# First layer's attention: max with zero on GpSimd, one more unit of lag, square split 320 to 1728 columns

## The reference, cut to what matters

```python
sq = q2 + swapaxes(k2) - 2.0 * einsum('bhqd,bhkd->bhqk', Q, K)
dist = sqrt(maximum(sq, 0.0))
W = (1e-4 + dist) ** (-2)
W = W / (1e-4 + sum(W, axis=-1, keepdims=True))
A = einsum('bhqk,bhkd->bhqd', W, V)
```

## Time and profile before

| | us |
|---|---|
| median of 3 runs | 7800.41 (7792.85 to 7807.29) |
| span of the profiled execution | 7789.6 |
| VectorE busy | 7317.2 (94%) |
| ScalarE busy | 7213.7 (93%) |
| TensorE busy | 4179.2 (54%) |
| GpSimd busy | 66.0 (1%) |
| stretch of the first layer's attention | 240 to 2720 |

### The profile page before, as it was taken

The page is one execution under the profiler, slowest core; times in us unless marked ns, Lnnn a source line. Parts: engine busy times, 40 slices in busy tenths (PEclk is TensorE's granted clock), DMA queues, the critical chain, the costliest instruction groups (busy, mean ns, idle before and its releaser), DMA issues. The chain is left out here.

```text
span 7789.6 us, 58667 instructions
## 1 busy us (share of the span) xinstructions
PE 4179.2 (54%) x17232; PEld 1286.2 (17%) x17232; DVE 7317.2 (94%) x6415; ACT 7213.7 (93%) x4385; POOL 66.0 (1%) x68
## 2 busy tenths in 40 slices
PE   6666666666766675444444444444444444444445
PEld 3221222222222141111111111111111111111112
DVE  7899999999999858999999999999999999999996
ACT  3799999999999836999999999999999999999996
POOL 0000000000000000000000000000000000000000
PEclk8888888888787886655656656655665655655667
DMA  3100000000000031000000000000000000000002
GB/s 127 39 17 12 16 16 12 16 12 16 12 17 11 28 129 49 10 6 6 10 6 6 10 6 6 10 6 6 10 6 6 10 6 6 10 6 6 10 2 67
DMA packets 113664, 148.32 MB, mean 19 GB/s; under 512 B 17038, under 2 KB 98857, under 8 KB 112634
## 3 DMA queue, kind: packets, MB, share of 16 engines
q1 hardware_dynamic: 104314, 138.54, 5.8%
q10 hardware_dynamic: 9216, 8.39, 0.3%
HBM read 91.55 MB, written 55.31 MB: 19 GB/s over the span
## 5 line engine op out<-in xcount | busy, mean ns | idle before, releaser
L716 PE MATMUL psS<-q_stack,k_stack 102*128 102x512 bf16 (+1 forms) x4096 | 1743.2, 521 | 1979.7 <-DVE work L1023 1128.6
L738 PE MATMUL psO<-work,v_tile 128*32 128x512 f32 x8192 | 1432.7, 822 | 1467.9 <-DVE work L1045 1451.8
L1023 DVE TENSOR_SCALAR work<-psS 128x1024 f32<-128x1024 f32 x1024 | 1203.6, 1219 | 104.7 <-PE psS L716 49.7
L907 DVE SCALAR_TENSOR_TENSOR work<-work,psS 128x1024 f32<-128x1024 f32 x1024 | 1244.5, 1216 | 41.9 <-ACT work L865 41.3
L1066 DVE TENSOR_TENSOR work<-work 128x2048 f32<-128x2048 f32 x512 | 1143.6, 2296 | 77.1 <-ACT work L985 76.8
L865 ACT ACTIVATE work<-psS 128x1024 f32<-128x1024 f32 x1024 | 1100.6, 1075 | 71.2 <-PE psS L716 46.1
L1030 DVE TENSOR_TENSOR work<-work 128x2048 f32<-128x2048 f32 x512 | 1147.7, 2283 | 0.0
L880 ACT ACTIVATE work<-work 128x2048 f32<-128x2048 f32 x512 | 1005.8, 1964 | 0.4 <-ACT ffn_out L797 0.4
L990 ACT ACTIVATE work<-work 128x4096 f32<-128x4096 f32 x256 | 923.9, 3609 | 27.4 <-DVE work L1066 23.6
L980 ACT ACTIVATE work<-work 128x4096 f32<-128x4096 f32 x256 | 910.8, 3606 | 31.2 <-DVE work L1030 21.7
L985 ACT ACTIVATE work<-work 128x2048 f32<-128x2048 f32 x512 | 935.9, 1898 | 1.4
(11 more groups left out here) (124 smaller groups left out, 2478.3 us busy)
## 6 DMA issues: line engine op xcount, KB each, us to landing
qk_parts<-work SPq DMA_DIRECT2D x64, 384.0 KB, 3.2
q_stack<-qk_parts SPq DMA_DIRECT2D x384, 64.0 KB, 2.2
k_stack<-qk_parts SPq DMA_DIRECT2D x384, 64.0 KB, 2.2
ffn_in<-xT_store SPq DMA_DIRECT2D x64, 128.0 KB, 2.5
y_store<-ffn_out ACTq DMA_DIRECT2D x64, 128.0 KB, 1.7
work<-y_store SPq DMA_DIRECT2D x8, 1024.0 KB, 12.2
work<-in_x SPq DMA_DIRECT2D x1, 4096.0 KB, 14.3
xn_store<-work SPq DMA_DIRECT2D x1, 4096.0 KB, 13.0
```

Of the source, the lines that this page charges most:

```text
L716: last = nc.tensor.matmul(m.psS[half][:, q * 512:(q + 1) * 512], m.k_stack[b][0:rows, kt * P:(kt + 1) * P], m.q_stack[b][0:rows, c:c + 512 ...
L738: last = nc.tensor.matmul(m.psO[b][VW * q:VW * (q + 1), :], m.v_tile[b][:, kt, :], ring[:, u % RING, q * 512:(q + 1) * 512], start=kt == 0 ...
L907: nc.vector.scalar_tensor_tensor(part, part, 0.5 / SHEP_EPS, m.psS[half][:, :], ALU.add, ALU.mult).then_inc(s_y, 1)
L1023: nc.vector.tensor_scalar(ring[:, u % RING, half * 1024:(half + 1) * 1024], m.psS[half][:, :], COS_MAX, -COS_MAX, ALU.min, ALU.max)\
```

## The change

In the first layer's attention the max with zero leaves VectorE's loop. GpSimd's queue gets it: for each unit it waits until both quotients of the unit are done and then applies min with the largest fp32 number and max with zero to the whole slot, in place. The two value copies of a head now stand in GpSimd's queue ahead of units 2 and 12. `LAG_INV`, `LAG_SQ` and `LAG_PV` each grow by one. `ACT_SQ` falls from 992 to 320, so that VectorE squares 1728 columns and ScalarE 320. GpSimd's loop over heads is written out for both layers, where a hardware loop ran over the inner heads.

```diff
-    LAG_PV = 5
-    LAG_INV, LAG_SQ = 2, 3
+    LAG_PV = 6
+    LAG_INV, LAG_SQ = 3, 4
-    ACT_SQ = 992
+    ACT_SQ = 320
...
+            def value_tile(h, b, first):
+                if not first:
+                    pool.wait_ge(s_pv, UNITS * h + KT * b + KT - UNITS)
+                nc.gpsimd.tensor_copy(m.v_tile[b][:, :, 0:DH], values[:, b, :, h, :]).then_inc(s_vt, 1)
+
             def head(h, first, last):
...
+                if L == 1:
+                    for b in range(B):
+                        value_tile(h, b, first)
+                else:
+                    for u in range(UNITS):
+                        if u == 2:
+                            value_tile(h, 0, first)
+                        if u == 12:
+                            value_tile(h, 1, first)
+                        c = UNITS * h + u
+                        pool.wait_ge(s_y, 2 * c + 2)
+                        slot = ring[:, u % RING, :]
+                        nc.gpsimd.tensor_scalar(slot, slot, F32_MAX, 0.0, ALU.min, ALU.max).then_inc(s_m, 1)
+            for h in range(HEADS):
+                head(h, h == 0, h == HEADS - 1)
...
                         if u < UNITS:
                             quotient(u, 0)
-                        if u <= UNITS and not (first and u < 1):
-                            dve.wait_ge(s_y, 2 * c)
-                            slot = ring[:, (u - 1) % RING, :]
-
-                            nc.vector.tensor_scalar(slot, slot, 0.0, None, ALU.max).then_inc(s_m, 1)
                         if u < UNITS:
                             quotient(u, 1)
```

More of the change, by code:

```diff
@@ L41 @@
 COS_MAX = 0.999
+F32_MAX = 3.4028234663852886e38
 PI = 3.141592653589793
```

## The result

The change makes the kernel slower: 7854.64 us, median of 4 runs (7847.75 to 7862.06), against 7799.3 for the kernel before (median of 4, 7792.85 to 7807.29). The ratio is 1.0074 with a 95% interval of 1.0059 to 1.0088, so +55 us where -84 was forecast. The predicted 7716 is off by 139 us and the sign is wrong.

The account below looks back on a forecast made before the run. VectorE, full at 4.57 us a unit, was taken to set the pace. The block was to fall from 76.81 to 74.1 us, -87 over 32 blocks, +3 for the end of the stage, from 7800.4: 7716 us, range 7630 to 8020.

Parts of the forecast that it names:

- the extras: VectorE's work between units: 0.39 us per hidden square and 1.21 for `dve_out`, 2.0 together where they were 2.6.
- a max of up to 2.4 us costs nothing: GpSimd's max lies beside the next two quotients, with 2.47 us until the next square; 2.0 us was assumed.
- 4.13 + e: Unit time with an extra e on VectorE, used when it exceeds 4.34 + e/2; 4.13 us is VectorE's own unit.
- the slow rival: GpSimd's max at 3.2 us and VectorE's square alternate and bound the unit at 5.1 us: 8003 us, chance 0.31.
- the forecast's own case: Likeliest case, chance 0.51: max of 2.0 us hidden beside quotients, block 74.1 us, total 7716 us.
- The wait between the quotients: VectorE idles before the second quotient because ScalarE's half isn't there: 0.21 us a unit, around 100 us in all.
- The plain unit: Attention unit without extras: 4.34 us at the fast clock (0.66), 4.62 at the lower (0.34), mixed to 4.44.
- the loop: From first quotient to next unit's second: T + g at least 5.68 us; T is the unit, g its quotients' distance.
- The lag: One unit more of lag costs 0; if its cover failed, 1 to 1.9 us a block, at most 60 us.
- The clock: TensorE's granted clock, 0.83 of full, keeps its share; leaving 0.8 to 0.9 would show the prediction wrong.
- went ahead of the slot's square: Rival: the max gets in before VectorE's square, which stands still; unit about 6.1 us, total 8590, chance 0.03.
- The drain: At the stage's end the last unit passes GpSimd and the longer square, and one more unit stands behind: +3 us.

Follow-up runs that it names:

- experiment 4: Changed kernel with GpSimd's max cut to 32 of the 2048 columns, waits and order kept: 7711.92 us, ratio 0.9893 to the kernel before.
- Experiments 1: Changed kernel with a block's two hidden squares moved from VectorE to ScalarE (kt 3 and 6): 7708.84 us, ratio 0.9892 to the kernel before.
- experiment 5: Kernel before with the three lags one larger and nothing else: 7794.03 us, ratio 0.9998 to the kernel before.
- experiment 3: Changed kernel with the hidden square ahead of the slot's square, behind the second quotient: 7860.87 us, ratio 1.0087 to the kernel before.
- experiment 7: Changed kernel with the hidden square replaced by a one-operand multiplication by 1.0 in place: 7830.15 us, ratio 1.0050 to the kernel before.
- experiment 8: Changed kernel with the hidden square written as relu(x) times x, second operand read from PSUM: 7743.09 us, ratio 0.9935 to the kernel before.

## Why the prediction was wrong, step by step

**The step that failed** is in the paragraph on the extras: "0.39 for each `hidden` square". I took it as 0.6 us of VectorE's time of which part falls into idle time. It was 2.3 us from start to start (1524.86 to 1527.16), because it stands directly behind the slot's square, with no quotient between them, and there GpSimd's max takes its turn. That a max of up to 2.4 us costs nothing, as the prediction has it, holds only where two quotients follow the square; at kt 4, 6 and 8 something else follows it. The prediction's own formula for an extra e too large for the idle time, 4.13 + e, gives 6.43 with e = 2.3, and units 4 and 6 took 6.43 and 6.42. Against the kernel with the short GpSimd operation (experiment 4) units 4 to 7 are 3.77 us longer, 120 us in 32 blocks, and unit 8, where the last product of `dve_out` waits in the same way, 0.59, which is 19: 139 us, the size of the miss. Experiments 1 and 4 remove the squares' wait in two different ways and land at 7709 and 7712. The rows for it were there: in the earlier trace rows a copy gets in between two products that stand back to back and the second pays. I priced that for the slow rival only, as a matter of GpSimd's speed, and I never asked which VectorE instruction stands behind the square in the forecast's own case.

**The rival that it resembles**, a bound on GpSimd, didn't happen. The max wasn't slow: 1.89 us alone (the first one of the stage), 1.76 behind a square, in the forecast's 1.6 to 2.1. It didn't bound the plain unit, and no slot's square waited in the steady state. What the list of rivals lacks is a fast operation in a place with no room. The last product of `dve_out` is the smaller case of it: 0.6 us a block, which the prediction also priced for the slow rival only.

**What held.** VectorE's square cost 1.87 from start to start (1522.99 to 1524.86), as worked out. The wait between the quotients appeared: 175.7 us idle, 174.7 of it released by ScalarE, where 100 was expected; with the short GpSimd operation 157 remain. The plain unit was forecast at 4.44 as a mean over the clock and measured at 4.41 in units 10 to 14. The granted clock there is 0.88 and not 0.83, and the prediction's mix of 4.34 and 4.62 gives 4.41 for it; in experiment 4 the clock there is 0.93, the mix 4.38 and the measured unit 4.38. What was wrong in it is that the low clock was spread evenly: the granted clock is 0.72 in units 4 to 9. The plain unit isn't even, though: the loop says g of the next unit is at least 2.68 less g of this one, and with VectorE never under 1.13 the units alternate, 4.13 and 4.56, whose mean is the 4.34 of the fast clock. The block without the missed term is 74.01 (experiment 4) for 74.1. The lag was free (experiment 5). The clock stayed within 0.8 to 0.9. GpSimd never went ahead of the slot's square: its record starts some 0.17 us after the square's. Where it came up before that square, in experiment 3, it did go ahead.

**Who waits for whom.** A VectorE product with two SBUF operands waited for the max (experiment 3, 3.64 us), a one-operand multiplication in the fast form did too (experiment 7, 2.11), and a product with one operand in PSUM did not (experiment 8, 0.68). SBUF — State Buffer of the Trainium skill (Who interferes with whom) says the same: VectorE instructions with two SBUF inputs contend with GpSimd instructions that read SBUF, `tensor_scalar` can run in a 2-port mode and then contends too, and an instruction with one SBUF input outside these modes does not. The max took 1.76 us behind a square and 1.89 alone; the estimate in the prediction from GPSIMD Engine Reference of the Trainium skill (Elementwise — side-by-side cycle accounting) was 1.76.

**The drain** was forecast at +3 and is 4.7 us longer. In it five slot squares follow one another, and the last max, recorded from 2756.07 for 3.54 us, gets in between two of them, as this row of the changed kernel shows: 11.12 us, where 5 x 1.87 + 0.08 would be 9.4.

```profile
2755.90 11.12 DVE L936 TENSOR_TENSOR work<-work 128x1728 f32<-128x1728 f32 x5
```

**What stays open.** In the changed kernel GpSimd got in between two neighbouring products 64 times of 64; in the earlier trace rows a copy that came up in the middle of a product was passed over by the next one. That row is the exception: of the 28 copies of the kernel before's second layer that came up during one product with another right behind it, 25 got in between and the second product took 2.48 us, and three were passed over. What decides it was not tried.

## What to carry to other kernels

When work moves to GpSimd, list every VectorE instruction that needs both operands from SBUF or runs in the fast form, and look at what stands directly behind each: here a short one behind a long one cost the whole of GpSimd's operation, fast as that was. Reading one operand from PSUM, or moving the short one to ScalarE, removed it. And when a step is taken out from between two others, compare the new distance of the consumers with that of their producers on the other engine; here the hidden squares moved alone gave 84 us against the kernel before, and another 77 came once ScalarE's two halves stood as close as VectorE's two quotients.

## What the runs showed of the hardware that I had not expected

- GpSimd's min and max over 128 x 2048 fp32 takes 1.89 us when nothing competes, against 1.22 for the max on VectorE. With a VectorE product ahead of it the record says 3.54 us: 1.78 from its start to the product's end, and 1.76 after it.
- The same 128 x 512 product on VectorE behind a long one: 2.38 us with both operands in SBUF, 0.68 with one in PSUM; as a one-operand multiplication in the fast form 2.11.
- A GpSimd operation of only 32 columns beside a square is recorded at 1.84 us and holds VectorE up by nothing that shows (L943 0.70 for 0.69).
